# The turn of the chosen weights before the row's store and the next attention's load in the DMA queue

## What is computed

```python
def _autocorrelation(Q, K, V):
    qf = jnp.fft.fft(q, axis=2)
    kf = jnp.fft.fft(k, axis=2)
    corr = jnp.fft.ifft(qf * jnp.conj(kf), axis=2).real
    topk = int(C * np.log(L))                       # 12 lags of 512
    w, idx = jax.lax.top_k(corr.transpose(0, 1, 3, 2), topk)
    w = jax.nn.softmax(w, axis=-1)
    for i in range(topk):
        g = jnp.minimum(idx[:, :, None, :, i] + pos, L - 1)
        out = out + w[:, :, None, :, i] * jnp.take_along_axis(v, g, axis=2)
...
x = x + _L0_xattn_ref(_layernorm(x, axis=-1), ctx_4096, ctx_4096)
x = x + _L0_ffn_ref(_layernorm(x, axis=-1), W, bias, A, Bf, coeffs, scales)
# _L0_ffn_ref: x @ W.T + bias + sum over 16 experts of w_e * (x @ A_e.T) @ Bf_e.T
```

## Time and profile before

| what | value |
|---|---|
| median of three runs | 2644.93 us |
| the three runs | 2644.93, 2644.93, 2651.17 us |
| the profiled execution | 2646.18 us |
| its span, first to last instruction | 2644.4 us |
| mean granted clock of TensorE | 0.984 |
| chain that ended last | PE 53%, POOL 22%, DVE 8%, DMA 7%, SyncE's queue 5% |
| share of the 16 DMA engines' time in the kernel's queue | 76.6%, mean 232 GB/s |

### The profile page before, as it was taken

How to read it: one execution, slowest core, us unless ns; L and a number is a source line. 1 busy time by engine, 2 the same in 40 slices (tenths; PEclk the granted TensorE clock), 3 DMA queues, 4 the chain that set the end, 5 groups by cost and what they waited for, 6 DMA issues and landing times.

```text
span 2644.4 us, 36606 instructions
## 1 busy us (share of the span) xinstructions
PE 2497.7 (94%) x12288; PEld 1559.9 (59%) x12288; DVE 1901.7 (72%) x4966; ACT 1055.7 (40%) x1906; POOL 2155.5 (82%) x1558
## 2 busy tenths in 40 slices
PE   4999866799999999999999999999999999999998
PEld 3655555566666656666666666666666666654444
DVE  5989989778787788777877788778876688645000
ACT  4788855533443343533443334533333233201000
POOL 5799999778998799988998899888998899654222
PEclk8999978899999999999999999999999999999999
DMA  9399998966788687966887687957786687758853
GB/s 325 99 261 269 269 244 198 231 192 209 254 266 228 219 252 238 277 203 210 258 270 210 217 275 248 271 181 236 253 250 172 219 265 243 199 203 301 268 180 114
DMA packets 550028, 613.19 MB, mean 232 GB/s; under 512 B 322640, under 2 KB 448720, under 8 KB 532176
## 3 DMA queue, kind: packets, MB, share of 16 engines
q1 hardware_dynamic: 549840, 610.86, 76.6%
HBM read 383.22 MB, written 151.00 MB: 202 GB/s over the span
## 4 chain that ended last, share of the span: by engine, by line
PE 53%; POOL 22%; DVE 8%; DMA 7%; SPq 5%; issue 4%; ACT 1%; POOLq 0%; DVEq 0%; ACTq 0%
PE f_ps L840 11%; PE f_ps L844 11%; PE f_ps L842 11%; PE a_ps L718 7%; PE a_ps L805 5%; PE a_ps L763 4%; POOL a_zu L1115 4%; POOL f_x1p L1115 4%; POOL a_rows L1115 3%; DMA a_w_lag<-a_w_row 2%; PE a_ps L821 2%; PE a_ps L820 2%; POOL a_zv L1115 2%; POOL a_zf L1115 2%; PE a_ps L768 1%
## 5 line engine op out<-in xcount | busy, mean ns | idle before, releaser
L840 PE MATMUL f_ps<-f_whi,f_hhi 128*128 128x512 f16 x2048 | 777.3, 380 | 5.6 <-issue 2.4
L844 PE MATMUL f_ps<-f_whi,f_hlo 128*128 128x512 f16 x2048 | 777.4, 380 | 0.0
L842 PE MATMUL f_ps<-f_wlo,f_hhi 128*128 128x512 f16 x2048 | 777.4, 380 | 0.0
L924 ACT ACTIVATE a_side<-a_ps 128x256 f32<-128x256 f32 (+1 forms) x320 | 128.0, 416 | 873.5 <-PE a_ps L805 698.4
L844 PEld LDWEIGHTS f_ps<-f_whi,f_hlo 128*128 128x128 f16 x2048 | 200.6, 98 | 242.3 <-issue 1.1
L842 PEld LDWEIGHTS f_ps<-f_wlo,f_hhi 128*128 128x128 f16 x2048 | 200.7, 98 | 230.8 <-issue 1.1
L840 PEld LDWEIGHTS f_ps<-f_whi,f_hhi 128*128 128x128 f16 x2048 | 200.7, 98 | 220.6 <-issue 6.7
L1115 POOL TENSOR_TENSOR a_prod<-a_prod,a_tf 128x512 f32<-128x512 f32 x128 | 160.2, 1273 | 138.7 <-DVE a_tf L1242 138.7
L1115 POOL TENSOR_TENSOR a_zv<-a_zv,a_tw 128x512 f32<-128x512 f32 x128 | 183.3, 1450 | 100.5 <-DVE a_tf L1242 100.5
L805 PE MATMUL a_ps<-inv,a_prod 128*128 128x256 f32 x1024 | 239.5, 388 | 25.6 <-POOL a_prod L1115 25.6
L1115 POOL TENSOR_TENSOR f_x1p<-f_x1p,f_y 128x512 f32<-128x512 f32 x128 | 172.7, 1381 | 101.0 <-DVE f_y L1242 101.0
(11 more groups left out here) (137 smaller groups left out, 5236.6 us busy)
## 6 DMA issues: line engine op xcount, KB each, us to landing
f_whi<-whi_scratch SPq DMA_DIRECT2D x128, 512.0 KB, 5.1
f_wlo<-wlo_scratch SPq DMA_DIRECT2D x128, 512.0 KB, 6.5
a_rows<-in_x_dram SPq DMA_DIRECT2D x62, 1024.0 KB, 8.7
vs<-in_ctx_dram SPq DMA_DIRECT2D x64, 512.0 KB, 6.2
xs<-in_x_dram SPq DMA_DIRECT2D x64, 512.0 KB, 8.0
parts_scratch<-a_so SPq DMA_DIRECT2D x64, 512.0 KB, 7.5
x_scratch<-a_rows SPq DMA_DIRECT2D x32, 1024.0 KB, 5.1
f_x1p<-x_scratch SPq DMA_DIRECT2D x32, 1024.0 KB, 6.8
```

Source lines behind the costliest of these rows:

```text
L840: nc.tensor.matmul(f_ps[:, t, :], h_hi[q][:, kq, rows_t], w_hi[u % WR][:, :, kq, :], start=(k == 0), stop=False)
L842: nc.tensor.matmul(f_ps[:, t, :], h_hi[q][:, kq, rows_t], w_lo[u % WR][:, :, kq, :], start=False, stop=False)
L844: mm = nc.tensor.matmul(f_ps[:, t, :], h_lo[q][:, kq, rows_t], w_hi[u % WR][:, :, kq, :], start=False, stop=(k == DB - 1))
L924: return nc.scalar.activation(out, source, ACT.Copy, **how)
```

## The change

In SyncE's window loop the two lines that issue the turn move up: from behind the row's store, the next attention load and three blocks that only early windows have, to ahead of the store.

```diff
@@ -668,6 +668,8 @@
                 if at and at[1] == 7:
                     for q in range(2):
                         load_h(at[0] + 1, q)
+                if turned_by_dma(w):
+                    turn_weights(w)
                 if r is not None:
                     store_x1(w, r)
                     if r % TB < TB - 1:
@@ -685,8 +687,6 @@
                     load_weights(0)
                     load_weights(1)
                     load_group(0)
-                if turned_by_dma(w):
-                    turn_weights(w)
                 if at:
                     load_weights(unit + 3)
                 load_v(w + 3)
```

## The result

The kernel before took 2644.93 us, the changed one 2667.36 us (2666.42 to 2670.03, four runs each). The ratio is 1.0082 with a 95% interval of 1.0064 to 1.010: slower by 22 us, where 23 less were forecast. The profiled execution of the changed kernel took 2666.42 us, its span is 2664.6.

A forecast was written before the change was run, and what follows sets the result against it. TensorE, busy 94%, was taken as the bound, waiting for turned weights behind the row's store. Stalls of 20.3 us plus 3.4 of slow clock, all other terms zero, gave 23.7 off: 2622 us, range 2618 to 2634.

The forecast's parts named there:

- the check of the total: Windows 14 to 62: 1766.20 us against 1742.40 undisturbed, an excess of 23.8; stalls and clock give 23.7.
- (a): Turns issued before store and attention load in row windows: all thirteen TensorE stalls go, 20.3 us, and 3.4 us of clock.
- the near row: Window 30, without a row: its second turn landed 4.0 us after the weights were ready, 4.5 before TensorE asks.
- Rival 1: Turns held by earlier-issued loads at positions 4 and 6: 17.9 us off, 2628, or 2634 with GpSimd's 6; chance 0.13.
- (b): Row's store behind both turns: 0.6 us late or less at positions 4 and 6, 5 at 3 and 5; cost nothing.
- The cover of 8 us: Between ScalarE having the row's high half ready (1024.72) and VectorE reading it (1032.74); absorbs a late store.
- Rival 3: Late store holds ScalarE, the high half, then VectorE's `f_rowlo`: 24 windows lose 48 us against 23.7 gained, 2669; chance 0.04.
- (c): Next row's attention load moves with the store, some 5 us later at positions 3 and 5; cost nothing.
- (d): Product weights, values and partial stores further back in the queue shift up to some 2 us; cost nothing.
- What is late next: GpSimd loses catch-up time but what follows keeps its place: zero cost, at the other end 1 us in six windows.
- The subtraction as it is written: GpSimd's idle before `a_zv` at position 5 less the stall before: 0.33 to 0.38 us left, 1.5 in the last pair.
- The sum: Whole kernel: 23.7 us off the profiled 2646.18 gives 2622.5; forecast 2622.

The follow-up runs named there:

- the small kernel: Kernels with only VectorE's subtraction against GpSimd's additions; subtraction up to 13.23 us with one-partition additions, 3.39 with those over 128 partitions.
- the version with the memsets: Changed kernel plus two one-element VectorE memsets ahead of `f_rowlo` at position 7; 2675.03 us, ratio 1.0111.
- the fastest one: Changed kernel plus one GpSimd wait on its own addition ahead of `a_zv`, a gap of 0.14 us; 2618.42 us, ratio 0.9894.

## Why the prediction was wrong

**What bounds the kernel, and the check of the total.** Right. The loss by stalls and clock was 23.8 us, and where nothing else came in its place the 48 windows took the 1742.4 us that the check gave (three versions to the hundredth).

**(a) The turns.** Right in what counts: start at w_low-0.73 at all positions, landing at +3.7 to +5.3 in 22 windows against the near row's 4.0; only the latest two, at position 6, come to +6.5 and +6.9 where 6.2 was estimated. No stall and no slow clock of that origin is left. Rival 1, turns held by earlier loads, did not come: the window in which they land latest still has 1.6 us.

**(b) The store.** Nearly right in its times at position 5 (in five of six windows landing at +7.3 to +7.4 and normalising at +7.4 to +7.5 where +7.1 was said; in window 35 at +8.6 and +8.7), too kind at position 6, where the store goes out some 1 to 3 us later than before in four of six windows, not 0.6 or less; at the latest, in window 44, it lands at +10.6 and ScalarE starts at +10.7. The cover of 8 us held: at position 7 `f_rowlo` starts at +18.5 to +18.8, as it did wherever no stall came before it (18.73). Rival 3 had the right end of the chain, `f_rowlo` with the selection behind it, and by chance nearly the right number, 2669, but its mechanism, a late store, did not occur in any window.

**(c), (d) Attention load and the rest of the queue.** Nothing, as said: no reader of theirs stands in TensorE's list, and the stretch of three versions is that of undisturbed windows.

**What is late next: the step that failed.** It asked whether GpSimd would make TensorE wait, by the room of 0.42 us before `a_zu` is loaded, and by the idle time left at position 5. Both came out as worked out: 0.32 to 0.36 us of idle in five windows and 1.48 in the last, and no wait of TensorE for `a_zu`. (The subtraction as it is written holds for four of the six pairs. In the pairs of windows 18 and 26, where the clock fell too, idle less stall is 4.56-3.17 = 1.39 and 4.60-4.13 = 0.47, not 0.33 to 0.38.) But from "VectorE still releases GpSimd there" it concluded "what follows keeps its place", and the window after position 6 was not looked at. There GpSimd is the later one in two of the six windows even before (no idle ahead of `a_zv` in windows 29 and 45), and with the last small stalls gone it is 0.1 to 0.7 us later than it was. The prediction priced that lateness by who waits for GpSimd, at up to 1 us a window. Its real price is paid in the duration of VectorE's instruction: 10.7 us of `f_rowlo`, of which 8.0 to 9.6 reach TensorE. The row was there to be seen: in the earlier trace rows `f_rowlo` takes 2.75 at 1032.74, where it takes 2.28 at position 5 and up to 3.45 at position 4, and GpSimd's `a_zv` pair takes 4.48 in the earlier trace rows where 2.49 is usual. Two engines lengthened each other's instructions wherever they met, and I took the durations as fixed.

The Trainium skill (SBUF — State Buffer, section "SBUF: two separate sides") has a rule that gives the likely reason: VectorE with two SBUF inputs and GpSimd share a port pair under an exclusive lock, held for one whole instruction, and the other "fully blocks". The prediction has no term for it. No row here shows a port, but the durations agree with the rule where GpSimd works on 128 partitions: 2.28 to 3.39 us in the small kernel, and in the kernel before 5.59 us where `f_rowlo` starts 1.07 us into an addition of 4.51, which leaves 3.44, and 3.44+2.28 = 5.72. They differ behind a one-partition instruction, where VectorE stood through nine further instructions, and in the two cases of 5.93 and 6.43 us; there the measurement decides.

**The sum.** With the side effect taken away the gain was 23.8 us in the 48 windows and 29.1 by the spans (2644.4 and 2615.3); of the other 5.3, 1.9 lie ahead of window 14 (its pair starts at 527.43 instead of 529.34) and 3.4 behind window 62; their cause was not looked into. The loss was 44.9 us, with no line in the sum. 23.8 off and 44.9 on make 21.1; the spans differ by 20.2 and the medians by 22.4. The chance of 0.04 for slower stood on a single mechanism. What was missing was not a wider range for its price but the view of every pair of instructions that overlap on these two engines and change their order.

## What to carry to other kernels

A stall can be what keeps two engines apart: before taking it away, note for the next engine behind it which of its instructions it will now overlap, and whether the durations of those instructions vary in the trace of before; variation between 2.28 and 2.75, or between 2.49 and 4.48, is the sign here that they meet. Where GpSimd runs a one-partition instruction followed by others without a wait, a short wait on its own result behind it (0.14 us) lets VectorE in, as it did in all six windows here, and so does doing that addition over all partitions, where the values of the other rows may be written. Prove the worth of both edits apart and together, since here the gap alone gave nothing, the turn alone cost 22 us, and together they gave 28.

## What the runs showed of the hardware

- A VectorE subtraction of 128x2048 with two inputs in SBUF that comes while GpSimd works takes its turn at GpSimd's next instruction, and GpSimd's then waits for it: 2.28 to 3.39 us in the small kernel with 128 partitions only. Beside a GpSimd addition of 4.51 us (128x2048) it took up to 5.59 in the kernel before, 6.34 in the version with the memsets.
- If it comes during a one-partition addition of GpSimd (0.71 us), more than about 0.3 us before its end, it gets no turn at the next boundaries. The wait ended ahead of the next one-partition addition (7.3 to 7.4 us), behind it (7.3 to 8.5) or only at GpSimd's first gap (10.5 to 10.8 and 12.9 to 13.2). The kernel showed the last in 20 windows and the first in one; what decides between them is open. At +0.30 and +0.31 both 7.3 and 12.9 occur.
- Without a wait for VectorE behind it, even a start 0.45 us after the end of the one-partition addition is shut out (7.26 us). Where GpSimd waits for VectorE, a start below the edge is let in. Up to +0.14 the records show a gap made by that wait (`zv` begins 0.16 after the subtraction); at +0.20 and +0.24 they show none (`zv` begins 0.03 before the addition's end, as in variant plain), so the gap alone does not explain it.
- Two `f_rowlo` outside position 7, 5.93 us in the version with the memsets and 6.43 in the fastest one, came in a run of GpSimd's additions on 128 partitions with no one-partition one ahead, got no turn at three boundaries and were let in ahead of the next one-partition addition, which took 2.8 us. So shutting out is not bound to the one-partition form alone. What does it there, and why the handing over fails behind one partition, is open.
- TensorE at a granted clock of 0.50 came after an idle time of 6.3 us and lasted 6.83 us by the records, in each of the five windows.
